# Attention scores as four 32-row products per query tile, one head to a PSUM bank

## The chip, the cores and the metric

The kernel runs on one core of one Trainium2 chip. The metric is the device time of one execution in microseconds (us). Time before: 1463.14 us, the median of 3 runs (1463.08 to 1464.67).

## What is computed

A cross-attention layer with a feed-forward part, and behind it a mixture of eight experts, for 4 x 2048 tokens of 512 numbers. The change touches only the scores of the attention:

```python
q = (x @ Wq + bq).reshape(B, N, 16, 32)      # B 4, N 2048: 16 heads of 32 numbers
k = (y @ Wk + bk).reshape(B, 77, 16, 32)     # 77 context rows for each of the 4 batches
scores = jnp.einsum('bnhd,bmhd->bhnm', q, k) / sqrt(32)
attn = softmax(scores, axis=-1)
out = einsum('bhnm,bmhd->bnhd', attn, v).reshape(B, N, 512)
x = x + relu(out @ W1 + b1) @ W2 + b2        # then layernorm, top-1 of 8 experts
```

## The kernel before

The tokens are worked in 16 blocks (`NBLK`) of 512 (`BLK`), each of 4 sub-tiles (`SUB`) of 128 tokens; four blocks in a row (`BPB`) share one context of `M` = 77 rows. Every large product is done in float32r as three products of split operands: high by high, high by low, low by high (`split3`, L599).

One block goes through these steps on TensorE: transposes of the normalised input (`XT`, L984), the queries (`Q`, L1016, four chunks of 128 features, so four heads each), the scores (`S`, L1042), transposes of the probabilities (`PT`, L1117), attention by values (`AV`, L1153), the hidden layer (`H`, L1201) and the output layer (`YA` and `Y`, L1223). The steps are written out by hand in one list (L273 to L532); every engine walks the same list and does its own part of each step, in that order. The scores of block b+1 are put between the output products of block b (L502 to L514): four groups g = 0 to 3, each a chunk of four heads, and behind each group a half of an output product, and for g = 0 and 1 also the queries of group g+2.

A group of scores before the change is four steps, one for each sub-tile s of 128 tokens. The keys stand in a tile `kbd` in which the four heads are laid out block-diagonally: rows 32h to 32h+31 hold the keys of head h in columns 77h to 77h+76, and zeros elsewhere. So one product of 128 rows by `SC` = 308 columns gives all four heads of a sub-tile, and three such products (L1042) fill one PSUM bank. There are 16 x 4 x 4 x 3 = 768 of them.

Behind them VectorE takes the negated maximum of each head (`dve_s`, L1051). In groups 0 and 2 (`ON_ACT`) ScalarE computes the exponentials and their sums head by head (`act_s`, L1084: 16 instructions of 77 columns per group). In groups 1 and 3 VectorE first subtracts the maximum (`dve_sub`, L1071), and ScalarE then does the whole group in one instruction (`act_soft`, L1092), with the sums on VectorE (L1100). VectorE then takes the reciprocals (`dve_sum`, L1105), GpSimd multiplies the probabilities by them (`pool_soft`, L1111), and TensorE transposes them. The transposes of the second pair of groups begin with two that need group 2 alone (`CA`), and these are the sixth and seventh transposing steps of a block (L283 to L288).

The eight PSUM banks are given out in the order of the list (L574 to L588): each step that writes a bank takes the one given up the longest ago and waits for its last reader (`own_bank`, L590).

`kbd` is zeroed by GpSimd at the start (L791), filled by ScalarE for the first context (`act_kcopy`, L815), and refilled from a DRAM copy of the split keys (`sp_kstore` L697, `sp_kload` L704) three times, by four DMAs each. On the queue of SyncE the load of W2 stands behind the store of the keys (L338, L339).

Of the kernel before, what the change touches and what calls it, by code (L numbers as in the profile page):

```python
# [27 lines left out]
P = 128  # L28
D = 512
# [21 lines left out]
SCP = (SC + 63) // 64 * 64  # L51
# [24 lines left out]
def xattn_moe_kernel(nc, A, out):  # L76
    region = nc.dram_tensor("region", [NE * REG + P, ROW], F32).ap()
    k_parts = nc.dram_tensor("k_parts", [P, 2, KD, NB * M], F32).ap()
# [28 lines left out]
    kbd, _ = sb("kbd", [P, 2, KD, SCP], F32R)  # L107
# [65 lines left out]
    k_hl = staged("k_hl", [P, 2, KD, NB * M], F32R)  # L173
# [15 lines left out]
    assert 4 * NE * D <= size([P, 2, KD, SCP], F32) + size([P, 2, NP, NC, P], F32)  # L189
# [54 lines left out]
    with ExitStack() as ctx:  # L244
        bank = [ctx.enter_context(nc.psum_tensor(f"bank{i}", [P, 512], F32)) for i in range(8)]

        def sem(name):
# [7 lines left out]
        st_k, st_v, ld_k, ld_v = sem("st_k"), sem("st_v"), sem("ld_k"), sem("ld_v")  # L255
# [8 lines left out]
            "act_wq dve_wq act_w1 pool_w1 act_w2 dve_w2 act_kbd dve_tri "  # L264
# [86 lines left out]
        step("VSTORE", 0)  # L351
        step("CONV_W1", 0)
# [3 lines left out]
        for s in range(SUB - 1):  # L356
            step("S", 0, 0, s)
        step("QLO", 0, 1)
        step("Q", 0, 2)
        step("S", 0, 0, SUB - 1)  # L360
        step("CONV_W1", 1)
        for s in range(SUB):
            step("S", 0, 1, s)
# [4 lines left out]
        for s in range(SUB):  # L368
            step("S", 0, 2, s)
# [3 lines left out]
        for s in range(SUB):  # L373
            step("S", 0, 3, s)
# [9 lines left out]
        for b in range(NBLK):  # L384
            last = b == NBLK - 1
            if (b + 1) % BPB == 0 and not last:
                step("KLOAD", (b + 1) // BPB)
# [75 lines left out]
            if last:  # L463
                step("GELU")
                step("PAD_LOAD")
                step("YA", b, 0)
                step("Y", b, 0)
                step("YA", b, 1)
                step("Y", b, 1)
                step("YA", b, 2)  # L470
                step("TT", b, 0)
                step("TTOUT", b, 0)
                step("Y", b, 2)
                step("TT", b, 1)
                step("TTOUT", b, 1)
                step("YA", b, 3)
                step("TT", b, 2)
                step("TTOUT", b, 2)
                step("Y", b, 3)
            else:  # L480
                prep = b - PREP0 if PREP0 <= b < PREP0 + NE else None
                step("DRAIN")
                step("YA", b, 0)
                for s in range(SUB):
                    step("XB", b + 1, s)
                step("Y", b, 0)
                for s in range(2):
                    step("XT", b + 1, s)
                step("YA", b, 1)
                for s in range(2, SUB):  # L490
                    step("XT", b + 1, s)
                if prep is not None:
                    step("E2_RAW", prep)
                    step("E1_RAW", prep)
                step("Y", b, 1)

                for m in range(2):
                    step("Q", b + 1, m)
                    step("QLO", b + 1, m)
                if prep is not None:  # L500
                    step("E2_HIGH", prep)
                for g, (first, y) in enumerate((("YA", 2), ("Y", 2), ("YA", 3), ("Y", 3))):  # L502
                    for s in range(SUB):
                        step("S", b + 1, g, s)
# [34 lines left out]
        def score_done(b, g, s):  # L539

            mine, name = (ON_ACT, "act_es") if g in ON_ACT else (ON_DVE, "dve_sub")
            return S[name], SUB * (len(mine) * b + mine.index(g)) + s + 1


        def group_of(p, i):
# [8 lines left out]
            "S": lambda b, g, s: score_done(b, g, s),  # L554
# [139 lines left out]
        def sp_kstore(sp):  # L694
            sp.wait_ge(S["act_k"], KD)
            sp.wait_ge(S["dve_k"], KD)
            sp.dma_start(k_parts, f32(k_hl[:])).then_inc(st_k, 16)  # L697

        def sp_kload(sp, i):
            sp.wait_ge(st_k, 16)  # L700
            sp.wait_ge(S["pe_s"], KD * SUB * BPB * i)
            for h in range(HG):
                q = slice(HD * h, HD * h + HD)
                sp.dma_start(f32(kbd[q, :, :, M * h:M * h + M]).rearrange("p s g k -> p (s g) k"),  # L704
                             k_parts[q, :, :, M * i:M * i + M].rearrange("p s g k -> p (s g) k")).then_inc(ld_k, 16)

# [16 lines left out]
        KLOADS, VLOADS = HG, len(PIECES)  # L723
# [36 lines left out]
        def sp_ebload(sp):  # L760
            sp.wait_ge(S["pe_s"], KD * SUB * NBLK)
# [45 lines left out]

        def act_kcopy(act):

            act.wait_ge(S["pool_zero"], 1)  # L810
            act.wait_ge(S["act_k"], KD)
            act.wait_ge(S["dve_k"], KD)
            for h in range(HG):
                q = slice(HD * h, HD * h + HD)
                act.activation(kbd[q, :, :, M * h:M * h + M], k_hl[q, :, :, 0:M], ACT.Identity).then_inc(S["act_kbd"], 1)  # L815
# [35 lines left out]
        def act_kp(act, m):  # L851
# [7 lines left out]
            act.activation(k_hl[:, 0, m, :], k_f[:, m, :], ACT.Identity).then_inc(S["act_k"], 1)  # L859

        def dve_klo(dve, m):
            dve.wait_ge(S["act_k"], m + 1)
            dve.tensor_tensor(k_hl[:, 1, m, :], k_f[:, m, :], f32(k_hl[:, 0, m, :]), ALU.subtract
                              ).then_inc(S["dve_k"], 1)
# [180 lines left out]
        def dve_s(dve, b, g, s):  # L1045

            dve.wait_ge(S["pe_s"], SUB * (KD * b + g) + s + 1)
            if b and s == 0 and g in ON_ACT:
                dve.wait_ge(S["act_es"], SUB * (len(ON_ACT) * (b - 1) + ON_ACT.index(g) + 1))
            p = grouped(of("S", b, g, s)[:, 0:SC], HG)  # L1050
            dve.tensor_reduce(mx[:, SUB * g + s, :], p, AX, ALU.max, negate=True).then_inc(S["dve_max"], 1)  # L1051
            if g in ON_DVE:
                if s:
                    dve_sub(dve, b, g, s - 1)
                if s == SUB - 1:
                    drip(1)
                    dve_sub(dve, b, g, s)
# [9 lines left out]
        def dve_sub(dve, b, g, s):  # L1067
            if b and s == 0:
                dve.wait_ge(S["pe_pt"], NC * NP * b)
            dve.wait_ge(S["dve_max"], SUB * (KD * b + g) + s + 1)  # L1070
            dve.tensor_tensor(grouped(probs(g)[:, s, :], HG), grouped(of("S", b, g, s)[:, 0:SC], HG),  # L1071
                              spread(mx[:, SUB * g + s, :], M), ALU.add).then_inc(S["dve_sub"], 1)

        def act_s(act, b, g, s):
            if g not in ON_ACT:
                return
            if b == 0 and s == 0:
                act.wait_ge(S["dve_tri"], 1)
            if b and s == 0:
                act.wait_ge(S["pe_pt"], NC * NP * b)  # L1080
                act.wait_ge(S["dve_rc"], KD * (b - 1) + g + 1)
            act.wait_ge(S["dve_max"], SUB * (KD * b + g) + s + 1)
            for h in range(HG):
                ins = act.activation(probs(g)[:, s, M * h:M * h + M], of("S", b, g, s)[:, M * h:M * h + M], ACT.Exp,  # L1084
# [4 lines left out]
        def act_soft(act, b, g):  # L1089
            if g in ON_DVE:  # L1090
                act.wait_ge(score_done(b, g, SUB - 1)[0], score_done(b, g, SUB - 1)[1])
                act.activation(probs(g), probs(g), ACT.Exp).then_inc(S["act_exp"], 1)  # L1092

        def dve_sum(dve, b, g):
            i = KD * b + g
            if g in ON_ACT:
                dve.wait_ge(score_done(b, g, SUB - 1)[0], score_done(b, g, SUB - 1)[1])
# [22 lines left out]
        def act_pt(act, b, pr, c):  # L1120
            j = NC * pr + c
            if b == 0 and j == 0:
                act.wait_ge(st_k, 16)
                act.wait_ge(S["act_kbd"], HG)
# [585 lines left out]
        def pool_store(pool, t):  # L1710
# [10 lines left out]
            "KCOPY": {"act": act_kcopy},  # L1721
# [3 lines left out]
            "KSTORE": {"sp": sp_kstore},  # L1725
# [6 lines left out]
            "KLOAD": {"sp": sp_kload},  # L1732
# [152 lines left out]
```

## Time and profile before

| | us |
|---|---|
| median of 3 runs | 1463.14 |
| the profiled execution | 1461.93 |
| its span | 1460.1 |
| TensorE busy (matmul) | 1439.2 |
| VectorE busy | 1037.0 |
| ScalarE busy | 756.9 |
| GpSimd busy | 416.0 |
| score products, L1042, 768 of them | 118.7 |

Busy time is the union of the recorded spans of an engine's instructions; a matmul's record reaches past the start of the next, so the distance between two starts, not the length of a record, is what one costs in a row. PE is TensorE's matmul, PEld its load of weights, DVE is VectorE, ACT ScalarE, POOL GpSimd, SPq the DMA issues of SyncE's queue.

### The profile page before, as it was taken

Reading aid. Unit: us, or ns where it says so; the run is one execution under the profiler, and the core shown is the slowest. Engines: PE = TensorE matmul, PEld = TensorE weight load, DVE = VectorE, ACT = ScalarE, POOL = GpSimd, SP = SyncE. Lnnn points to the kernel's source line nnn. Section 1 sums busy time; section 2 is a strip of 40 time slices with the busy share of each in tenths; the row PEclk is TensorE's granted clock in tenths of the full one; section 3 lists DMA queues with packets and bytes.
Section 4 is the critical chain, followed back from the end, with each engine's and each line's share of the span. In section 5 each row is a group of like instructions: output and inputs, shape, how many; then the busy total and the mean of one; then the engine's idle time right before and its main releaser. Section 6 shows DMA issues by size and latency. Waiting matters only on the chain.

```text
span 1460.1 us, 23469 instructions
## 1 busy us (share of the span) xinstructions
PE 1439.2 (99%) x7704; PEld 1203.9 (82%) x7704; DVE 1037.0 (71%) x2522; ACT 756.9 (52%) x2096; POOL 416.0 (28%) x306
## 2 busy tenths in 40 slices
PE   8999999999999999999999999999999999999997
PEld 6788887888788888888787888888887878788996
DVE  6768586776868685867768685858576675748666
ACT  6746353645445363536454453635363544547885
POOL 3422222212121312222221213122222213108875
PEclk9999999999999999999999999999999999999999
DMA  8210202121120303130211201130202012357984
GB/s 294 85 58 1 88 1 73 38 79 55 36 88 22 102 7 103 28 99 30 81 43 37 87 23 58 43 91 1 87 1 87 1 44 73 145 174 255 305 257 149
DMA packets 70339, 121.60 MB, mean 83 GB/s; under 512 B 21851, under 2 KB 30308, under 8 KB 69197
## 3 DMA queue, kind: packets, MB, share of 16 engines
q1 hardware_dynamic: 59421, 86.41, 19.5%
q0 software_dynamic: 10800, 33.70, 6.0%
q8 instruction: 65, 1.06, 0.3%
q14 instruction: 53, 0.43, 0.1%
HBM read 75.19 MB, written 46.40 MB: 83 GB/s over the span
## 4 chain that ended last, share of the span: by engine, by line
PE 96%; DVE 2%; ACT 1%; issue 1%; DMA 0%; POOLq 0%; POOL 0%; SPq 0%; DVEq 0%
PE bank L1201 24%; PE bank L1223 24%; PE bank L1016 12%; PE bank L1153 8%; PE bank L1042 7%; PE bank L1623 4%; PE bank L1117 4%; PE bank L1661 3%; PE bank L1607 2%; PE bank L1298 2%; PE bank L984 2%; PE bank L1276 1%; DVE actH L1134 1%; ACT actH L1128 1%; PE bank L847 1%
## 5 line engine op out<-in xcount | busy, mean ns | idle before, releaser
L1223 PE MATMUL bank<-w,actH 128*128 128x512 f32 x1536 | 372.1, 393 | 0.0
L1201 PE MATMUL bank<-actA,w 128*128 128x512 f32 x1536 | 370.4, 394 | 0.0
L1201 PEld LDWEIGHTS bank<-actA,w 128*128 128x128 f32 x1536 | 284.2, 188 | 61.0
L1223 PEld LDWEIGHTS bank<-w,actH 128*128 128x128 f32 x1536 | 283.0, 188 | 55.9
L1111 POOL TENSOR_TENSOR E<-E,rc 128x1232 f32<-128x1232 f32 x64 | 144.1, 2252 | 423.3 <-DVE rc L1105 423.3
L1373 POOL DMA_INDIRECT region<-rows,pos x64 | 63.7, 996 | 456.6 <-DVE pos L1367 418.2
L1208 ACT ACTIVATE actH<-bank,b 128x512 fp32r<-128x512 f32 x128 | 88.4, 691 | 189.4 <-PE bank L1201 189.4
L1016 PE MATMUL bank<-actA,wq 128*128 128x512 f32 x768 | 182.4, 390 | 0.0
L1084 ACT ACTIVATE E<-bank,mx 128x77 f32<-128x77 f32 x512 | 157.8, 362 | 34.9 <-DVE mx L1051 34.9
L1016 PEld LDWEIGHTS bank<-actA,wq 128*128 128x128 f32 x768 | 144.1, 188 | 30.3 <-issue 0.5
L1030 DVE SCALAR_TENSOR_TENSOR actQ<-bank,bq,actQ 128x512 fp32r<-128x512 f32 x64 | 48.0, 750 | 158.5 <-ACT actQ L1025 158.5
L1213 DVE TENSOR_TENSOR actH<-bank,actH 128x512 fp32r<-128x512 f32 x128 | 88.2, 689 | 55.7 <-ACT bank L1209 55.0
L1153 PE MATMUL bank<-actH,vbd 128*128 128x512 f32 (+1 forms) x480 | 122.0, 400 | 4.2 <-DVE actH L1134 4.2
L1084 ACT ACTIVATION_READ_ACCUMULATOR E<-bank,mx 128x1 f32 x512 | 124.5, 243 | 0.0
L1042 PE MATMUL bank<-kbd,actQ 128*128 128x308 f32 x768 | 118.7, 303 | 0.0
L1042 PEld LDWEIGHTS bank<-kbd,actQ 128*128 128x128 f32 x768 | 113.9, 188 | 5.7 <-issue 0.5
L1051 DVE TENSOR_REDUCE mx<-bank 128x4 f32<-128x308 f32 x256 | 110.4, 471 | 6.8 <-PE bank L1042 6.8
L1025 ACT ACTIVATE actQ<-bank,bq 128x512 fp32r<-128x512 f32 x64 | 44.1, 689 | 125.1 <-PE bank L1016 125.0
L1153 PEld LDWEIGHTS bank<-actH,vbd 128*128 128x128 f32 (+1 forms) x480 | 86.5, 188 | 25.7 <-DVE actH L1134 6.9
L1134 DVE TENSOR_TENSOR actH<-bank,actH 128x512 fp32r<-128x512 f32 (+1 forms) x160 | 98.7, 676 | 11.5 <-ACT actH L1128 11.5
L1006 POOL TENSOR_TENSOR rows<-rows,b2bc 128x512 f32<-128x512 f32 x64 | 84.7, 1335 | 52.5 <-DMA rows<-in_x 43.7
L989 ACT ACTIVATE actA<-bank 128x512 fp32r<-128x512 f32 x64 | 34.7, 596 | 107.7 <-PE bank L984 107.7
(172 smaller groups left out, 2108.3 us busy)
## 6 DMA issues: line engine op xcount, KB each, us to landing
rowB<-region SPq DMA_DIRECT2D x71, 258.0 KB
xn<-in_x SPq DMA_DIRECT2D x64, 256.0 KB, 2.9
rows<-in_x SPq DMA_DIRECT2D x64, 256.0 KB, 3.5
w_raw<-in_W SPq DMA_DIRECT2D x2, 2048.0 KB, 10.5
e_raw<-in_E SPq DMA_DIRECT2D x16, 256.0 KB, 3.2
region<-padrow SPq DMA_DIRECT2D x9, 258.0 KB, 2.2
e_parts<-e_high SPq DMA_DIRECT2D x8, 256.0 KB, 2.0
e_parts<-e_low SPq DMA_DIRECT2D x8, 256.0 KB, 2.3
```

What stands on the lines that cost most here:

```text
L1006: nc.gpsimd.tensor_tensor(r, r, b2bc[:], ALU.add).then_inc(S["pool_xb"], 1)
L1016: mm = pe.matmul(p[:], w, a, start=k == 0 and j == 0, stop=k == KD - 1 and j == 2)
L1042: mm = pe.matmul(p[:, 0:SC], q, k, start=j == 0, stop=j == 2)
L1051: dve.tensor_reduce(mx[:, SUB * g + s, :], p, AX, ALU.max, negate=True).then_inc(S["dve_max"], 1)
L1084: ins = act.activation(probs(g)[:, s, M * h:M * h + M], of("S", b, g, s)[:, M * h:M * h + M], ACT.Exp, bias=mx[:, SUB * g + s, h:h + 1], a ...
L1111: nc.gpsimd.tensor_tensor(e, e, r, ALU.mult).then_inc(S["pool_p"], 1)
L1134: dve.tensor_tensor(actH[0:CH[c], 1, j % SLOTS, :], of("PT", b, pr, c)[0:CH[c], :], f32(actH[0:CH[c], 0, j % SLOTS, :]), ALU.subtract).the ...
L1153: mm = pe.matmul(p[:], v, w, start=c == mine[0] and t == 0, stop=c == mine[-1] and t == 2)
L1201: mm = pe.matmul(p[:], w, a, start=k == 0 and j == 0, stop=k == KD - 1 and j == 2)
L1208: act.activation(actH[:, 0, m, :], p[:], ACT.Relu, bias=b1[:, m:m + 1])
L1213: dve.tensor_tensor(actH[:, 1, m, :], of("H", b, m)[:], f32(actH[:, 0, m, :]), ALU.subtract).then_inc(S["dve_h"], 1)
L1223: mm = pe.matmul(p[:], a, w, start=m == 0 and j == 0, stop=m == MF - 1 and j == 2)
```

## The change

`kbd` is gone. The split keys stay in `k_hl`, now a tile of its own with `KW` = 320 columns for all four contexts, its 12 last columns zeroed. The zeroing of `kbd`, the copies into it, its store and its twelve loads are gone, with their semaphores; the load of W2 moves behind the loads and the store of the first values on SyncE's queue.

A group of scores is now four steps by head, not by sub-tile. Each takes a bank, but TensorE does the whole group at the last of them: for each of the 4 sub-tiles and each of the 3 split products, four products of 32 rows by `KS` = 78 columns, one per head, each to the bank of its head. So 48 products per group where there were 12, and 3072 in all. The one increment of the semaphore comes after the last. VectorE and ScalarE read by head: the maxima of the four sub-tiles of one head, the subtraction likewise, the exponentials in as many instructions of the same size.

```diff
-        step("KSTORE")
-        step("W2_LOAD")
         step("CONV_WQ", 1)
         step("VP", 0)
-        step("KCOPY")
...
         step("VSTORE", 0)
+        step("W2_LOAD")
         step("CONV_W1", 0)
...
-            if (b + 1) % BPB == 0 and not last:
-                step("KLOAD", (b + 1) // BPB)
...
-            z(f32(kbd[:])).then_inc(S["pool_zero"], 1)
+            z(f32(k_hl[:, :, :, NB * M:KW])).then_inc(S["pool_zero"], 1)
...
-        def pe_s(pe, b, g, s):
-            p = own_bank(pe, "S", b, g, s)
-            if s == 0:
-                pe.wait_ge(S["dve_q"], KD * b + g + 1)
-                pe.wait_ge(S["act_kbd"], HG)
-                if b >= BPB:
-                    pe.wait_ge(ld_k, 16 * KLOADS * (b // BPB))
-            for j, (q, k) in enumerate(split3([actQ[:, h, g, P * s:P * s + P] for h in range(2)],
-                                              [kbd[:, h, g, 0:SC] for h in range(2)])):
-                mm = pe.matmul(p[:, 0:SC], q, k, start=j == 0, stop=j == 2)
+        def pe_s(pe, b, g, h):
+
+
+            own_bank(pe, "S", b, g, h)
+            if h < HG - 1:
+                return
+            pe.wait_ge(S["dve_q"], KD * b + g + 1)
+            if b == 0:
+                pe.wait_ge(S["pool_zero"], 1)
+                pe.wait_ge(S["dve_k"], g + 1)
+            i = b // BPB
+            for s in range(SUB):
+                for j, (q, k) in enumerate(((0, 0), (0, 1), (1, 0))):
+                    for h in range(HG):
+                        r = slice(HD * h, HD * h + HD)
+                        mm = pe.matmul(of("S", b, g, h)[:, KS * s:KS * s + KS], actQ[r, q, g, P * s:P * s + P],
+                                       k_hl[r, k, g, M * i:M * i + KS], start=j == 0, stop=j == 2)
             mm.then_inc(S["pe_s"], 1)
...
+        def dve_s(dve, b, g, h):
+
+            dve.wait_ge(S["pe_s"], KD * b + g + 1)
...
+            dve.tensor_reduce(maxima(g, h), scores(b, g, h), AX, ALU.max, negate=True).then_inc(S["dve_max"], 1)
```

## Rows read from the trace of the kernel before

**Rows 1.** The page: TensorE's busy time, and its granted clock in 40 slices.
```profile
PE 1439.2 (99%) x7704; PEld 1203.9 (82%) x7704; DVE 1037.0 (71%) x2522; ACT 756.9 (52%) x2096; POOL 416.0 (28%) x306
...
PEclk9999999999999999999999999999999999999999
```

**Rows 2.** The page: the chain that ended last, shares by engine and line.
```profile
PE 96%; DVE 2%; ACT 1%; issue 1%; DMA 0%; POOLq 0%; POOL 0%; SPq 0%; DVEq 0%
PE bank L1201 24%; PE bank L1223 24%; PE bank L1016 12%; PE bank L1153 8%; PE bank L1042 7%; PE bank L1623 4%; PE bank L1117 4%; PE bank L1661 3%; PE bank L1607 2%; PE bank L1298 2%; PE bank L984 2%; PE bank L1276 1%; DVE actH L1134 1%; ACT actH L1128 1%; PE bank L847 1%
```

**Rows 3.** Groups by line and shape: score products, count | busy us, mean ns | idle before.
```profile
L1042 PE MATMUL bank<-kbd,actQ 128*128 128x308 f32 x768 | 118.7, 303 | 0.0
L1042 PEld LDWEIGHTS bank<-kbd,actQ 128*128 128x128 f32 x768 | 113.9, 188 | 5.7 <-issue 0.5 <-DVE actQ L1030 0.4
```

**Rows 4.** Timeline of PE around group 0, block 8: start us, length us, count.
```profile
650.94 5.60 PE L1016 MATMUL bank<-actA,wq 128*128 128x512 f32 x24
656.38 1.85 PE L1042 MATMUL bank<-kbd,actQ 128*128 128x308 f32 x12
658.07 2.92 PE L1223 MATMUL bank<-w,actH 128*128 128x512 f32 x12
```

**Rows 5.** Timeline of PE and PEld, 149 us: four products of 16 rows, L1312.
```profile
148.75 0.39 PE L1201 MATMUL bank<-actA,w 128*128 128x512 f32 x1
149.07 0.42 PE L1312 MATMUL bank<-ident,csb 16*128 16x16 f32 x4
149.41 1.43 PE L1201 MATMUL bank<-actA,w 128*128 128x512 f32 x5
...
149.07 0.32 PEld L1312 LDWEIGHTS bank<-ident,csb 16*128 16x128 f32 x4 [0.35 <-issue]
149.41 1.23 PEld L1201 LDWEIGHTS bank<-actA,w 128*128 128x128 f32 x6
```

**Rows 6.** The line L1312 over the whole run: count, duration min/median/max, idle before.
```profile
L1312 PEld LDWEIGHTS bank<-ident,csb x60: 132/136/138, 149.1 to 1265.4; 16*128 16x128 f32 x60
L1312 PE MATMUL bank<-ident,csb x60: 207/208/229, 149.1 to 1265.4; 16*128 16x16 f32 x60
...
  issue: 5.3, 15
```

**Rows 7.** Timeline of PE, block 8: the shortest pairs of load and product.
```profile
635.33 0.24 PE L1347 MATMUL bank<-cum,ones 128*128 128x8 bf16 x4
635.43 3.00 PE L1201 MATMUL bank<-actA,w 128*128 128x512 f32 x12
```

**Rows 8.** Timeline of PEld: two full weight loads whose products have one column.
```profile
621.45 0.30 PEld L1398 LDWEIGHTS bank<-onesf,e_acc 128*128 128x128 f32 x2
621.67 2.62 PEld L1201 LDWEIGHTS bank<-actA,w 128*128 128x128 f32 x12
```

**Rows 9.** Timeline of all engines from group 3 of block 8 to its transposes.
```profile
675.16 1.85 PE L1042 MATMUL bank<-kbd,actQ 128*128 128x308 f32 x12
...
675.78 0.90 DVE L1051 TENSOR_REDUCE mx<-bank 128x4 f32<-128x308 f32 x2 [0.23 <-PE bank L1042]
...
676.85 2.93 PE L1223 MATMUL bank<-w,actH 128*128 128x512 f32 x12
...
678.14 0.85 DVE L1071 TENSOR_TENSOR E<-bank,mx 128x308 f32<-128x308 f32 x2
678.91 0.24 DVE L1105 RECIPROCAL rc<-sm 128x16 f32<-128x16 f32 x1
...
679.24 2.25 POOL L1111 TENSOR_TENSOR E<-E,rc 128x1232 f32<-128x1232 f32 x1 [1.34 <-DVE rc L1105]
679.62 3.22 PE L1117 MATMUL bank<-ident,E 128*128 128x128 f32 x28
```

**Rows 10.** Timeline of PE, block 0: its sixth transposing step.
```profile
45.23 1.06 PE L1117 MATMUL bank<-ident,E 128*128 128x128 f32 x8 [0.18 <-POOL E L1111]
```

**Rows 11.** Timeline of the first 75 us: work removed or moved by the change.
```profile
0.75 2.23 POOL L790 MEMSET kbd<- 128x2560 f32 x1 [0.29 <-POOLq L1878]
...
18.91 6.02 PE L1016 MATMUL bank<-actA,wq 128*128 128x512 f32 x24
...
19.82 2.97 ACT L815 ACTIVATE kbd<-k_hl 32x616 fp32r<-32x616 f32 x4 [0.88 <-DVE k_hl L863]
20.17 0.43 SPq L664 DMA_DIRECT2D w_raw<-in_W  x1
...
36.95 0.42 SPq L729 DMA_DIRECT2D v_parts<-v_hl  x1
```

**Rows 12.** DMA issues: KB, us to landing; and the line that first reads W2.
```profile
w_raw<-in_W SPq DMA_DIRECT2D x2, 2048.0 KB, 10.5
kbd<-k_parts SPq DMA_DIRECT2D x12, 77.0 KB, 2.5
...
L924 ACT ACTIVATE w<-w_raw x4: 1062/1075/1103, 66.4 to 73.8; 128x1024 fp32r<-128x1024 f32 x4
```

More of the change, by code:

```diff
@@ L50 @@
 SC = HG * M
-SCP = (SC + 63) // 64 * 64
+KS = M + 1
+KW = (NB * M + 63) // 64 * 64
 NP = KD // 2
@@ L188, in xattn_moe_kernel @@
     b2e = at("b2e", [P, NE, D], F32, vbd_at)
-    assert 4 * NE * D <= size([P, 2, KD, SCP], F32) + size([P, 2, NP, NC, P], F32)
+    assert 4 * NE * D <= size([P, 2, KD, KW], F32) + size([P, 2, NP, NC, P], F32)
     o = [w2_at]
@@ L351, in xattn_moe_kernel @@
         step("VSTORE", 0)
+        step("W2_LOAD")
         step("CONV_W1", 0)
         step("Q", 0, 1)
-        for s in range(SUB - 1):
-            step("S", 0, 0, s)
+        for h in range(HG):
+            step("S", 0, 0, h)
         step("QLO", 0, 1)
         step("Q", 0, 2)
-        step("S", 0, 0, SUB - 1)
         step("CONV_W1", 1)
-        for s in range(SUB):
-            step("S", 0, 1, s)
+        for h in range(HG):
+            step("S", 0, 1, h)
         step("QLO", 0, 2)
@@ L367, in xattn_moe_kernel @@
         step("SUM", 0, 0)
-        for s in range(SUB):
-            step("S", 0, 2, s)
+        for h in range(HG):
+            step("S", 0, 2, h)
         step("QLO", 0, 3)
@@ L372, in xattn_moe_kernel @@
         step("SUM", 0, 1)
-        for s in range(SUB):
-            step("S", 0, 3, s)
+        for h in range(HG):
+            step("S", 0, 3, h)
         step("EXP", 0, 3)
@@ L502, in xattn_moe_kernel @@
                 for g, (first, y) in enumerate((("YA", 2), ("Y", 2), ("YA", 3), ("Y", 3))):
-                    for s in range(SUB):
-                        step("S", b + 1, g, s)
+                    for h in range(HG):
+                        step("S", b + 1, g, h)
                     if prep is not None and g == 0:
@@ L692, in sp_xload @@
                 sp.dma_start(rows[b % 2][:, s, 0:D], src).then_inc(ld_x[b % 2][s], 16)
[L694 to L705, printed above, removed]
         def sp_vload(sp, i, part):
@@ L721, in sp_vload @@
                              ).then_inc(ld_v, 16)
-        KLOADS, VLOADS = HG, len(PIECES)
+        VLOADS = len(PIECES)
         def sp_vstore(sp, i):
@@ L760, in sp_ebload @@
         def sp_ebload(sp):
-            sp.wait_ge(S["pe_s"], KD * SUB * NBLK)
+            sp.wait_ge(S["pe_s"], KD * NBLK)
             sp.wait_ge(S["pe_av"], 3 * NP * NBLK)
@@ L806, in dve_masks @@
             dve.tensor_copy(ones[:], c_raw[:, P:2 * P]).then_inc(S["dve_tri"], 1)
[L808 to L815, printed above, removed]
         def pe_gate(pe):
@@ L1045, in dve_s @@
[L1045 to L1051, printed above, removed]
+        def pe_s(pe, b, g, h):
[9 more added lines that the diff above has]
+                for j, (q, k) in enumerate(((0, 0), (0, 1), (1, 0))):
+                    for h in range(HG):
+                        r = slice(HD * h, HD * h + HD)
+                        mm = pe.matmul(of("S", b, g, h)[:, KS * s:KS * s + KS], actQ[r, q, g, P * s:P * s + P],
+                                       k_hl[r, k, g, M * i:M * i + KS], start=j == 0, stop=j == 2)
+            mm.then_inc(S["pe_s"], 1)
@@ new lines, in scores, with maxima @@
+        def scores(b, g, h):
+            return of("S", b, g, h)[:, 0:SUB * KS].rearrange("p (s k) -> p s k", s=SUB)[:, :, 0:M]
+        def maxima(g, h):
+            return mx[:, SUB * g:SUB * g + SUB, h]
+        def dve_s(dve, b, g, h):
+            dve.wait_ge(S["pe_s"], KD * b + g + 1)
+            if b and h == 0 and g in ON_ACT:
+                dve.wait_ge(S["act_es"], HG * (len(ON_ACT) * (b - 1) + ON_ACT.index(g) + 1))
+            dve.tensor_reduce(maxima(g, h), scores(b, g, h), AX, ALU.max, negate=True).then_inc(S["dve_max"], 1)
@@ L1052, in dve_s @@
             if g in ON_DVE:
-                if s:
-                    dve_sub(dve, b, g, s - 1)
-                if s == SUB - 1:
+                if h:
+                    dve_sub(dve, b, g, h - 1)
+                if h == HG - 1:
                     drip(1)
-                    dve_sub(dve, b, g, s)
+                    dve_sub(dve, b, g, h)
         def probs(g):
@@ L1065, in by_head, with dve_sub, act_s @@
             return ap.rearrange("p s (h k) -> p s h k", h=HG)
-        def dve_sub(dve, b, g, s):
-            if b and s == 0:
+        def dve_sub(dve, b, g, h):
+            if b and h == 0:
                 dve.wait_ge(S["pe_pt"], NC * NP * b)
[L1070 to L1074, printed above, removed]
+            dve.wait_ge(S["dve_max"], HG * (KD * b + g) + h + 1)
+            dve.tensor_tensor(probs(g)[:, :, M * h:M * h + M], scores(b, g, h), spread(maxima(g, h), M), ALU.add
+                              ).then_inc(S["dve_sub"], 1)
+        def act_s(act, b, g, h):
             if g not in ON_ACT:
                 return
-            if b == 0 and s == 0:
+            if b == 0 and h == 0:
                 act.wait_ge(S["dve_tri"], 1)
-            if b and s == 0:
+            if b and h == 0:
                 act.wait_ge(S["pe_pt"], NC * NP * b)
                 act.wait_ge(S["dve_rc"], KD * (b - 1) + g + 1)
-            act.wait_ge(S["dve_max"], SUB * (KD * b + g) + s + 1)
-            for h in range(HG):
-                ins = act.activation(probs(g)[:, s, M * h:M * h + M], of("S", b, g, s)[:, M * h:M * h + M], ACT.Exp,
+            act.wait_ge(S["dve_max"], HG * (KD * b + g) + h + 1)
+            for s in range(SUB):
+                ins = act.activation(probs(g)[:, s, M * h:M * h + M], scores(b, g, h)[:, s, :], ACT.Exp,
                                      bias=mx[:, SUB * g + s, h:h + 1],
```

28 lines of the change are left out of this document (11 added, 17 removed).

## Prediction

> **What bounds the kernel now.** I read the page's busy times first: TensorE has 1439.2 us of 1460.1, at a granted clock of 1.0 (the 2.4 GHz level) in every slice [rows 1]. The chain that ended last runs 96% over TensorE, 7% of it through the score products [rows 2]. So TensorE's own sequence is the time: what a score group costs there counts in full, 64 times (16 blocks, 4 groups), and a saving on another engine counts nothing unless TensorE waits for it. The groups by line give 768 score products and a weight load for each, with 0.0 and 5.7 us of idle time before them [rows 3]. The timeline of one group gives the pace: 24 query products take 5.44 us from first start to the first score (0.227 each), the 12 score products 1.69 us to the next start (0.141 each) [rows 4]. The 204 columns between 512 and 308 cost 0.086 us, 0.42 ns a column. Loads are hidden here.
>
> **What a group costs after.** Before, from the start of the last product ahead to the first start behind: 0.23 + 1.69 = 1.92 us. After, 48 products with 48 loads stand there. Four terms:
>
> *Entry.* The only products of few rows in this trace are the transposes of 16 rows. The last full product ahead of them starts at 148.75, their first load at 149.07: 0.32 us, where a full product would have followed in 0.23, and the load would have run beside the product ahead. PEld shows the gap as 0.35 us ended by "issue" [rows 5], 5.3 us in 15 such places [rows 6]. No semaphore is named. I read it as the array emptying before products with another number of rows. 0.32 us.
>
> *First load.* Two full loads whose products have a single column start 0.22 us apart over two, 0.11 each [rows 8]: that is a 128-column load's own pace. Nothing hides the first one: 0.11 us.
>
> *Exit.* The four small transposes take 0.42 us to the end of the last record, which is 0.21 long [rows 5, 6], so the last starts at 149.28; the next full load comes 0.13 us later at 149.41 [rows 5]. A product of 78 columns is 62 columns longer, 0.03 us, and the load before the first full product again costs 0.11. Together 0.27 us.
>
> *Pace.* 47 steps of p. The trace has no products of 32 rows in different row groups, so p is bounded from both sides. Below: four bf16 products with their loads start within 0.10 us, 0.025 each [rows 7]; nothing in the trace is issued faster. Above: one load after the other, 0.11 us each [rows 8]. Between them lies the pace of the 16-row loads, all in the same rows: (0.32 - 0.136) / 3 = 0.061 us [rows 5, 6]. The change alternates the four heads, so four consecutive loads go to four different sets of 32 rows and four consecutive products to four banks. If these sets work side by side, four loads take the time of one: 0.11 / 4 = 0.028. I take 0.028, next to the lowest row, because [rows 4] already show a load running beside a product under way. If in each set the load also had to wait for that set's own product (78 x 0.42 ns = 0.033 us), p would be 0.143 / 4 = 0.036.
>
> The group costs 0.70 + 47p: 2.02 us at 0.028, so +0.10 us per group, +6 us over 64. At 0.025 it is 1.88 (-3 us), at 0.036 2.39 (+30 us).
>
> The Trainium skill, "TensorE: Matmul & The Clock Gate", LDWEIGHTS, says that a load's time is its columns divided by 1.2 GHz, whatever its rows: an estimate of 107 ns here. The full loads agree (0.11), the 16-row ones don't (0.061), so by the rule alone the one-at-a-time case below would sit at its dear end. Part 3 of the same page says that loads overlap products under way only in a differing row group; no run here shows it yet.
>
> **The wait that is added.** Before, VectorE could begin a group after the first of four banks. Now all four are complete only at the end of the group. Ahead of groups 0 to 2 nothing waits that closely. Group 3 is different. Before: its products start at 675.16, the first maximum at 675.78 (0.62 us), the last subtraction ends at 678.99, reciprocals of group 2 behind them at 678.91, then GpSimd 679.24 to 681.49, which is 6.33 us after 675.16 [rows 9]. Queued behind the maxima on VectorE are thus the subtractions and the reciprocals on which group 2's probabilities wait, and behind the subtractions ScalarE's exponentials of group 3. TensorE starts transposing at 679.62, 0.109 apart ((3.22 - 0.27) / 27), and its 21st product, the first that needs group 2, comes at 681.80 [rows 9]: 0.31 us of slack, the same pattern in blocks 1 to 15. In block 0 there is none, TensorE waits 0.18 us there [rows 10].
>
> After: the last product starts 0.11 + 1.32 = 1.43 us behind the group's first load; its record is some 0.24 us (between 0.208 for 16 columns and 0.303 for 308 [rows 3, 6]), and 0.04 to VectorE as before (0.28 + 0.30 to 0.62). So the maxima start at 1.71 instead of 0.62, 1.09 us later, and GpSimd ends at 7.42. TensorE, whose way to the transposes is 1.70 instead of 1.69, is there at 6.65. With 0.1 us of hand-over it waits 0.87 us per block, 14 us over 16 blocks. A longer p moves both sides alike. What is late next, VectorE's low parts of the transposed probabilities, is some 1.1 us later too and TensorE 0.9, so at most 0.2 us more per block; I leave that in the range.
>
> **What is removed or moved.** All at nothing. GpSimd's 2.23 us memset and ScalarE's 2.97 us of copies lie beside other work: the query products run from 18.91 to 24.8 while the copies are made [rows 11]. The twelve reloads (2.5 us to land) are issued once group 3 of a context's last block is through, half a block's output and hidden products before the next scores; TensorE's idle time names none of them [rows 3, 12]. W2's load moves on SyncE's queue from 20.17 to about 37.4, behind the value loads and their store at 36.95; it needs 10.5 us, so it lands by 48, and its first reader starts at 66.4 [rows 11, 12]. The token loads behind it are 0.4 us later. If the cover of W2 were gone it would cost what it lands past 66.4; 18 us are left. The number and size of VectorE's and ScalarE's instructions stays.
>
> **Sum.** +6 +14 = +20 us on the profiled execution's 1461.9 (its span and 1.8 us around it), 1482; the median of the runs shown lies 1.2 us above the profiled one, so 1483.
>
> **Rivals.**
>
> *One load at a time, in the small rows' pace* (p = 0.061): for it, the only products of few rows in the trace go at this pace; against, they all use the same rows. 0.70 + 2.87 = 3.57 us, +1.65 x 64 = +106, with the wait +120: 1583.
>
> *The change doesn't do what it says*: products of different heads don't run side by side at all and each load costs its full 0.11 (p = 0.11). 5.87 us, +253, with the wait +267: 1730. For it: a full load is no cheaper for a product of one column.
>
> *Faster*: the entry and exit gaps belong to those transposes alone and not to the number of rows. Then entry is 0.23, exit 0.14 and the first load hidden: 0.37 + 47 x 0.025 = 1.55 us, -0.37 x 64 = -24, with the wait of 14 us: 1453. It decides from a group cost below 1.92 - 0.22 = 1.70 us, where the saving passes the wait. Against it: [rows 6] show the same gap in all 15 places, both ways.
>
> The Trainium skill, "TensorEngine Tiling (Array Packing)", Key Properties, says that changing the tiling mode drains the engine and that different tiles load and multiply in parallel. By the first, the faster rival falls; by the second, both dear rivals do. The first agrees with the gaps of 0.32 and 0.13 us; no row shows the second.
>
> **How the numbers follow.** Side by side, with the drain (p 0.025 to 0.036: 1474 to 1507, likeliest 1483): 0.55. One at a time or partly so (1507 to 1600): 0.16. No gain from rows (about 1730): 0.13. Faster by over 0.2% (down to 1453): 0.10. Within 0.2%, about what a measurement of this kernel can tell from no change, between these: 0.06. The range reaches from 1455 to 1592, leaving out the dearest rival and the ends of its neighbours. Faster 0.10, same 0.06, slower 0.84.
>
> **What would show it.** In the changed kernel: the distance from the last full product to the first score load (0.32), from the last score product to the next full load (0.16), the start-to-start pace of the 3072 products (0.028), the first maximum of group 3 at 1.7 us behind its first load, and an idle time of TensorE at the transposing line, put down to GpSimd, of some 14 us where there are 0.2. A pace of 0.06 or more makes the prediction far too low; gaps like any other product's make it too high.

## The result, and the profile after

The changed kernel takes 1477.35 us (median of 4 runs, 1476.07 to 1480.55) against 1463.11 for the kernel before on the same chip: ratio 1.0099, 95% interval 1.0080 to 1.0118, so 14 us slower. Its profiled execution has a span of 1474.3 us, 14.1 more than before.

The page of the changed kernel: busy times and the granted clock in 40 slices, to be read against [rows 1].

```profile
PE 1437.9 (98%) x10008; PEld 1181.5 (80%) x10008; DVE 1039.7 (71%) x2522; ACT 750.5 (51%) x2092; POOL 413.5 (28%) x306
...
PEclk9999999999999999999999999999999999999999
```

TensorE has 2304 more products, is busy 1.3 us less and spans 14.1 us more. The time went into idle time of TensorE, not into its products. The groups by line and shape of the changed kernel (count | busy us, mean ns | idle us before and its releaser), where [rows 3] had 118.7 us:

```profile
L1020 PE MATMUL bank<-k_hl,actQ 32*128 32x78 f32 x3072 | 98.4, 280 | 2.6 <-ACT E L1069 1.3 <-DVE actQ L1002 1.3
```

**One group.** The timeline of TensorE in the changed kernel, group 0 of block 8 (start us, length us), against [rows 4]:

```profile
659.88 5.60 PE L988 MATMUL bank<-actA,wq 128*128 128x512 f32 x24
665.42 1.54 PE L1020 MATMUL bank<-k_hl,actQ 32*128 32x78 f32 x48
666.88 3.01 PE L1207 MATMUL bank<-w,actH 128*128 128x512 f32 x12
669.73 2.88 PE L988 MATMUL bank<-actA,wq 128*128 128x512 f32 x12
```

24 query products take 5.54 us to the first score product, 0.10 more than before: the entry, 0.32 instead of 0.23. The group takes 1.46 to the next start instead of 1.69. The twelve output products behind it take 2.85. In the kernel before the same twelve start at 658.07 [rows 4], and the next row of its timeline is

```profile
660.83 1.52 PE L1016 MATMUL bank<-actA,wq 128*128 128x512 f32 x6
```

so they took 2.76 there: after the change the first of them waits 0.09 for its load. The whole piece, from the first query product to the start behind the twelve output products, is 5.44 + 1.69 + 2.76 = 9.89 us before and 5.54 + 1.46 + 2.85 = 9.85 after. A group costs 0.04 us less than before, where I forecast 0.10 more.

**Group 3 and its consumers.** The timeline of all engines of the changed kernel in block 8, against [rows 9]:

```profile
684.10 1.54 PE L1020 MATMUL bank<-k_hl,actQ 32*128 32x78 f32 x48
...
685.69 0.87 DVE L1036 TENSOR_REDUCE mx<-bank 128x4 f32<-128x308 f32 x2 [1.16 <-PE bank L1020]
...
688.01 0.85 DVE L1056 TENSOR_TENSOR E<-bank,mx 128x308 f32<-128x308 f32 x2
688.44 2.35 PE L1102 MATMUL bank<-ident,E 128*128 128x128 f32 x20
688.78 0.24 DVE L1090 RECIPROCAL rc<-sm 128x16 f32<-128x16 f32 x1
688.90 1.24 ACT L1077 ACTIVATE E<-E 128x1232 f32<-128x1232 f32 x1 [2.02 <-DVE E L1056]
...
689.11 2.25 POOL L1096 TENSOR_TENSOR E<-E,rc 128x1232 f32<-128x1232 f32 x1 [2.24 <-DVE rc L1090]
...
691.50 1.06 PE L1102 MATMUL bank<-ident,E 128*128 128x128 f32 x8 [0.72 <-POOL E L1096]
```

The maxima start 1.59 us behind the group's first product (0.62 before), and VectorE itself now waits 1.16 us. GpSimd ends at 691.36, and the sixth transposing step, which could have followed at 690.62, starts at 691.50: 0.72 us recorded as idle, 0.88 between starts. What follows on TensorE, first in the kernel before, then in the changed one:

```profile
682.67 0.60 PE L1276 MATMUL bank<-ident,rows 128*128 128x128 f32 x4
683.17 3.68 PE L1153 MATMUL bank<-actH,vbd 128*128 128x512 f32 x15
```

```profile
692.40 0.60 PE L1260 MATMUL bank<-ident,rows 128*128 128x128 f32 x4
692.76 3.70 PE L1137 MATMUL bank<-actH,vbd 128*128 128x512 f32 x15
696.29 0.60 PE L1260 MATMUL bank<-ident,rows 128*128 128x128 f32 x4
```

Before, the first value product stood 0.50 us behind the start of the four transposes ahead of it, now 0.36: a little is given back there. From the first transpose to the first value product it is 683.17 - 679.62 = 3.55 us before and 692.76 - 688.44 = 4.32 after, 0.77 more in a block. The line's waits over the run, from its own view (idle us, times):

```profile
  POOL E L1096: 12.2, 16
```

**Block 0.** The timeline of TensorE in the changed kernel:

```profile
25.80 1.54 PE L1020 MATMUL bank<-k_hl,actQ 32*128 32x78 f32 x48
...
30.84 1.54 PE L1020 MATMUL bank<-k_hl,actQ 32*128 32x78 f32 x48 [0.56 <-ACT E L1069]
...
36.62 1.54 PE L1020 MATMUL bank<-k_hl,actQ 32*128 32x78 f32 x48 [1.29 <-DVE actQ L1002]
...
41.70 1.54 PE L1020 MATMUL bank<-k_hl,actQ 32*128 32x78 f32 x48 [0.77 <-ACT E L1069]
...
49.69 1.07 PE L1102 MATMUL bank<-ident,E 128*128 128x128 f32 x8 [1.41 <-POOL E L1096]
```

From the first scores to that sixth transposing step it takes 23.89 us; before it took 45.23 - 24.77 = 20.46. Each group here waits until all of its four banks are free, or for low parts of queries that are behind the group's maxima on VectorE.

**The balance.** The first scores start 1.0 us later, at 25.80 instead of 24.77 (not shown to be the change's: the kernel before with two steps moved, below, starts as late); block 0 takes 3.4 us more; the transposes of 15 blocks at 0.77 are 11.6 us; 60 groups at -0.04 are -2.4. That makes 13.6 of the 14.1, taking block 8 for all of blocks 1 to 15.

### The profile page after: what moved, and what is told of

Its sections match the earlier page's. It is cut to its first block, busy times and chain, and to the rows that moved or that the text cites. A ratio compares the mean times of both kernels' runs of the same rounds, so it can differ in the third digit from the quotient of the medians.

```text
span 1474.3 us, 28075 instructions
## 1 busy us (share of the span) xinstructions
PE 1437.9 (98%) x10008; PEld 1181.5 (80%) x10008; DVE 1039.7 (71%) x2522; ACT 750.5 (51%) x2092; POOL 413.5 (28%) x306
## 4 chain that ended last, share of the span: by engine, by line
PE 90%; DVE 5%; POOL 2%; issue 1%; ACT 1%; DMA 0%; POOLq 0%; SPq 0%; DVEq 0%; ACTq 0%
PE bank L1185 24%; PE bank L1207 22%; PE bank L988 11%; PE bank L1137 8%; PE bank L1020 6%; PE bank L1607 4%; PE bank L1645 3%; POOL E L1096 2%; PE bank L1591 2%; PE bank L1282 2%; PE bank L956 2%; DVE mx L1036 2%; DVE E L1056 2%; PE bank L1102 2%; PE bank L1260 1%
## 5 line engine op out<-in xcount | busy, mean ns | idle before, releaser
L1207 PE MATMUL bank<-w,actH 128*128 128x512 f32 x1536 | 378.0, 397 | 0.0
L1020 PEld LDWEIGHTS bank<-k_hl,actQ 32*128 32x128 f32 x3072 | 91.0, 186 | 25.7 <-issue 25.7
L1020 PE MATMUL bank<-k_hl,actQ 32*128 32x78 f32 x3072 | 98.4, 280 | 2.6 <-ACT E L1069 1.3
L1102 PE MATMUL bank<-ident,E 128*128 128x128 f32 (+1 forms) x640 | 78.1, 273 | 12.2 <-POOL E L1096 12.2
```

Of the source, the lines that this page charges most:

```text
L1020: mm = pe.matmul(of("S", b, g, h)[:, KS * s:KS * s + KS], actQ[r, q, g, P * s:P * s + P], k_hl[r, k, g, M * i:M * i + KS], start=j == 0, s ...
L1102: mm = pe.transpose(p[0:CH[c], P * s:P * s + P], E[:, pr, s, P * c:P * c + CH[c]], ident[:])
L1207: mm = pe.matmul(p[:], a, w, start=m == 0 and j == 0, stop=m == MF - 1 and j == 2)
```

## Experiments

Each was timed beside the kernel before on the same chip; "ratio" is to that, with its 95% interval. They ran on three chips, where the kernel before took 1463.9, 1459.5 and 1459.8 us, so kernels timed on different chips are compared by ratio.

### The wait without the products

```diff
-            p = own_bank(pe, "S", b, g, s)
-            if s == 0:
...
+            own_bank(pe, "S", b, g, s)
+            if s < SUB - 1:
+                return
...
+            for s in range(SUB):
...
+            mm.then_inc(S["pe_s"], SUB)
```

> The kernel before with its 128-row products, but all four sub-tiles of a group done at the last of the four steps, with one increment behind the last product: the wait of the change without its products. Theory (the loss of the change is the later start of group 3 on VectorE, and bank waits in block 0; the products themselves cost nothing): the maxima start some 1.9 us behind the group's first product, against 0.62 before and 1.6 in the changed kernel, so TensorE waits about 1.0 us per block at the transposes, 16 us, and block 0 loses some 3 us at its banks: about 1481, no faster than the changed kernel. Rival (the loss is in the small products and the gaps around them): 1463, like before.

Measured: 1488.91 us, ratio 1.0170 (1.0153 to 1.0187), +25 us. The timeline of TensorE of this kernel, block 8 and then block 0:

```profile
693.47 1.85 PE L1044 MATMUL bank<-kbd,actQ 128*128 128x308 f32 x12
...
697.92 2.35 PE L1119 MATMUL bank<-ident,E 128*128 128x128 f32 x20
701.16 1.07 PE L1119 MATMUL bank<-ident,E 128*128 128x128 f32 x8 [0.89 <-POOL E L1113]
```

```profile
28.56 1.85 PE L1044 MATMUL bank<-kbd,actQ 128*128 128x308 f32 x12
33.94 3.42 PE L1044 MATMUL bank<-kbd,actQ 128*128 128x308 f32 x12 [3.53 <-ACT E L1086]
```

The wait of the change is there with the old products: 0.89 us recorded, 1.06 between starts (3.24 from 697.92 against 20 x 0.109), a little more than in the changed kernel because the group itself is longer. 15 x (1.06 - 0.11), with what the changed kernel gives back behind it (0.88 - 0.77) taken off, are 14 us, near the forecast of 16. The other 8 us over the forecast are in block 0, and come with my edit: its list has group 0's last step behind the third query chunk, so the whole group moved there (28.56 against 24.77), and group 1 behind it waits 3.53 us for banks. Behind that wait its twelve products take 3.42 us and not 1.85, because the granted clock fell there (us, TensorE busy (count), granted clock, DMA share, GB/s):

```profile
33.00:39.80 6.80, 5.86 (x19) 0.50 0.38 81
```

So part of the 8 us is clock and not waiting. The rival, that the loss lies in the small products, falls: the loss at the transposes is there without them.

### Taking the wait away

```diff
                     for h in range(HG):
                         step("S", b + 1, g, h)
+                        if g == 3 and h == 1:
+                            step("SUM", b + 1, 2)
...
-                    if g:
+                    if g in (1, 2):
                         step("SUM", b + 1, g - 1)
```

> The changed kernel with the reciprocals of group 2 (and with them GpSimd's product) put between the maxima of the second and the third head of group 3, in blocks 1 to 15. If the wait at the transposes is the only one, it goes and 15 x 0.78 = 12 us come back: about 1465. Theory as the trace is read: GpSimd then ends in time, but ScalarE's exponentials of group 3 still stand ahead of the copies of the transposed probabilities, so the first value product waits in its place (about 0.6 to 0.8 us per block): 1474 to 1478, under 4 us gained.

Measured: 1479.44 us, ratio 1.0104 (1.0087 to 1.0121). The timeline of TensorE, block 8:

```profile
689.43 3.22 PE L1104 MATMUL bank<-ident,E 128*128 128x128 f32 x28
...
693.85 3.70 PE L1139 MATMUL bank<-actH,vbd 128*128 128x512 f32 x15 [0.77 <-DVE actH L1120]
```

The 28 transposes run through, and the first value product waits 0.77 us instead. So the theory holds that the wait only moves. I had expected it between the changed kernel's time and up to 4 us less; it came out at or slightly above the changed kernel (ratio 1.0104 against 1.0099, within the intervals).

With the exponentials of group 3 moved as well:

```diff
-                    step("EXP", b + 1, g)
+                    if g < 3:
+                        step("EXP", b + 1, g)
...
                 step("PT", b, 0, c)
+                if b and c == 2:
+                    step("EXP", b, 3)
```

> The same, and the exponentials of group 3 put behind the third copy of transposed probabilities on ScalarE, in blocks 1 to 15. Theory: both consumers are then in time, the 12 us come back: 1464 to 1467, with no idle time of TensorE at the transposes or the value products outside block 0. Rival (something else than these two queues delays TensorE after group 3): above 1472.

Measured: 1472.47 us, ratio 1.0061 (1.0044 to 1.0078): some 5.5 us regained, not 12, at the edge of what the rival said.

```profile
685.40 3.22 PE L1107 MATMUL bank<-ident,E 128*128 128x128 f32 x28
688.46 0.60 PE L1265 MATMUL bank<-ident,rows 128*128 128x128 f32 x4
689.26 3.70 PE L1142 MATMUL bank<-actH,vbd 128*128 128x512 f32 x15 [0.20 <-DVE actH L1123]
```

The value products start 0.80 us behind the transposes' last group, 0.44 more than the 0.36 of the changed kernel (692.40 to 692.76): still a wait, now on VectorE.

> The kernel before with the same two moves. It has 0.3 us of slack at both places, so nothing is to be gained: 1463, within 1 us. If it gains as much as the changed kernel does by them, the moves are worth something by themselves and say nothing about the change.

Measured: 1469.78 us, ratio 1.0043 (1.0027 to 1.0060): not equal but slower, by 6 us. The two moves cost the kernel before 0.3 to 0.4 us per block. In block 8, 0.14 of it is at the first value product (0.64 us behind the four transposes ahead of it, against 0.50) and 0.19 at the eighth transposing step, which needs group 3's probabilities (1.66 us behind the start of six value products, against 1.47 in the kernel before): the late exponentials make the copies and the sums behind them late. So by themselves they are a loss; together with the change's late maxima they are the smaller of two losses. Against this kernel, the changed one with the same moves is only 2.7 us slower. Its start tells what the scatter of a start is: nothing ahead of block 1 differs from the kernel before, and yet its first queries start at 19.93 where [rows 11] have 18.91:

```profile
19.93 6.04 PE L1021 MATMUL bank<-actA,wq 128*128 128x512 f32 x24
```

Two more moves, to see whether the waits that are left can be taken away too:

```diff
-                    drip(DRIP.get(kind, 0))
+                    drip(0 if kind == "Y" and i[1] == 3 or kind == "PT" and i[1] == 0 and i[2] < 2 else DRIP.get(kind, 0))
...
+        step("QLO", 0, 2)
         for h in range(HG):
             step("S", 0, 1, h)
-        step("QLO", 0, 2)
```

> The changed kernel with the early reciprocals and the late exponentials, and two more moves: VectorE's statistics of the block before (0.69 us) go behind its low parts of the first three transposed chunks, and in block 0 the low part of the third query chunk goes ahead of group 1's maxima. Theory: the wait of 0.33 us per block at the first value product goes (5 us) and 1.3 us of block 0, from 1472.5: about 1466, no better than the kernel before, since 2 us of block 0 remain and the groups themselves gain only 0.03 us each. Rival (VectorE is full there, the wait only moves to the next consumer): 1471 or more.

Measured: ratio 1.0065 (1.0051 to 1.0079), no gain over the version before it. Its waits of TensorE (idle us in total, times, longest):

```profile
PE bank L1025 <- ACT E L1074: 2.5, 2, 1.9
PE bank L1107 <- POOL E L1101: 2.4, 15, 0.2
```

The wait at the first value product is gone; in its place the eighth transposing step waits for group 3's probabilities (2.4 us recorded in 15 places; in the timeline 1.78 us from the start of six value products, against 1.49 in the version before: 0.3 lost), and in block 0 a bank wait of 1.9 us stands where the queries' low part stood. Behind that wait the granted clock also fell in this execution (0.51 from 43.9 to 47.3 us), so that six 512-column products took 4.37 us where the changed kernel's take 2.71. The rival was right: around group 3 VectorE has no room, and what is taken from one consumer is missing at the next. No version beat the kernel before.

### What entering and leaving small products costs

```diff
+            if s == 0:
+                pe.matmul(p[:, 0:M + 1], actQ[0:HD, 0, g, 0:P], kbd[0:HD, 0, g, 0:M + 1], start=True, stop=True)
```

> The kernel before with one more product in each of the 64 groups, ahead of the twelve: 32 rows by 78 columns, into the first bank, overwritten right behind (its result is not used). Theory (entering and leaving 32-row products empties the array): 0.32 us from the last full product to it, 0.21 from it to the next full load and 0.11 for that load, where 0.23 stood: +0.41 us, 64 times, +26: about 1489. Rival (a small product costs only its own load or columns, 0.03 to 0.11 us): 1465 to 1470.

Measured: ratio 1.0186 (1.0170 to 1.0201), +27 us, 0.42 per group. The timeline of TensorE and the line's own view:

```profile
690.51 0.30 PE L1041 MATMUL bank<-kbd,actQ 32*128 32x78 f32 x1
690.74 1.95 PE L1044 MATMUL bank<-kbd,actQ 128*128 128x308 f32 x12
692.53 2.93 PE L1225 MATMUL bank<-w,actH 128*128 128x512 f32 x12
```

```profile
L1041 PE MATMUL bank<-kbd,actQ x64: 270/299/300, 25.2 to 1261.3; 32*128 32x78 f32 x64
...
  issue: 22.4, 63
```

The twelve products behind it take 1.79 us instead of 1.69: 0.10 for their first load. A single 32-row product costs as much as three score products of 308 columns. So entry and exit, 0.42 us together, are paid each time TensorE goes from 128 rows to 32 and back, 64 times here, for one product as for 48.

### The pace inside a group

```diff
-            for s in range(SUB):
+            for h0, s in [(h0, s) for h0 in (0, 2) for s in range(SUB)]:
...
-                    for h in range(HG):
+                    for h in (h0, h0 + 1):
```

> The changed kernel with the heads alternated two at a time: all products of heads 0 and 1, then all of heads 2 and 3; same 48 products, banks and increment. Theory (what sets the pace is one load of 0.112 us in each set of rows, and sets work side by side): 24 steps of 0.112 instead of 12, +1.34 us per group, +86: about 1563. Rival (the products are issued at a pace of their own, 0.028 each): 1477, as with four.

Measured: 1572.51 us, ratio 1.0771 (1.0754 to 1.0787), +113. The forecast was +86 on top of the change's 14, so 100.

The same with `for h0 in range(HG)` and `(h0,)`:

> The changed kernel with one head after the other: twelve products of head 0, then of head 1 and so on, all else as it is. Theory (a load costs 0.112 us in its rows, whatever its number of rows): 48 steps, +4.0 us per group, +258: about 1735. Rival (small loads go at the 0.061 us of the 16-row transposes): 48 x 0.061 = 2.9 against 1.34, +1.6 us per group, +102: about 1579.

Measured: 1798.9 us, ratio 1.2321 (1.2302 to 1.2340), +339. The forecast was 258 and 14. Timelines of TensorE, two heads at a time, then one:

```profile
645.85 2.45 PE L1020 MATMUL bank<-k_hl,actQ 32*128 32x78 f32 x48
648.23 4.60 PE L1207 MATMUL bank<-w,actH 128*128 128x512 f32 x12
```

```profile
650.79 5.29 PE L1020 MATMUL bank<-k_hl,actQ 32*128 32x78 f32 x48
656.02 5.17 PE L1207 MATMUL bank<-w,actH 128*128 128x512 f32 x12
```

Two things come together. *The groups*: 2.38 us to the next start with two heads, against 1.46 with four, +0.92 and not +1.34. Between the two halves the queue reaches ahead: the products of the second pair begin while those of the first are still under way, since they use other rows. In the timeline the pace falls out as 48 products in 2.45 - 0.28 = 2.17 us. So sets of rows do work side by side. One set by itself shows its pace in the run with one head at a time: eight loads of head 0, and seven of them, in two windows of its timeline of weight loads,

```profile
650.79 0.96 PEld L1020 LDWEIGHTS bank<-k_hl,actQ 32*128 32x128 f32 x8 [0.35 <-issue]
650.79 0.85 PEld L1020 LDWEIGHTS bank<-k_hl,actQ 32*128 32x128 f32 x7 [0.35 <-issue]
```

are 0.11 us apart. Within a set a load and its product take 0.11 us, and not the 0.061 of the rival: the first theory, with an overlap between sets that I had not foreseen. *The clock*: the output products behind take 4.60 us instead of 2.85. The windows of these stretches (core 0: us, TensorE busy (count), granted clock, DMA share, GB/s), two heads at a time:

```profile
645.90:648.20 2.30, 2.30 (x49) 1.00 0.00 0
648.30:652.70 4.40, 4.40 (x12) 0.61 0.00 0
```

In a full-speed stretch an output product takes 0.227 us, here up to 0.427: the 1.2 GHz level. Over the run the line's mean goes from 397 ns in the changed kernel to 433 with two heads and 485 with one (the groups by line and shape, in this order):

```profile
L1207 PE MATMUL bank<-w,actH 128*128 128x512 f32 x1536 | 378.0, 397 | 0.0
```

```profile
L1207 PE MATMUL bank<-w,actH 128*128 128x512 f32 x1536 | 423.7, 433 | 0.0
```

```profile
L1207 PE MATMUL bank<-w,actH 128*128 128x512 f32 x1536 | 492.2, 485 | 0.0
```

The clock explains what the pace doesn't: with two heads 59 us (64 x 0.92) over the changed kernel's 14 leave 40. The output products are busy 423.7 - 378.0 = 46 us longer than in the changed kernel and the queries 3.5; against that, VectorE has more time, and TensorE waits 7.2 us less at the transposes (5.0 against 12.2) and 2.6 less at the scores. That makes 40. With one head the mean clock is 0.90 and the groups themselves run partly at the lower level, so its total gives no clean price. Where the clock stayed up, a group takes 4.22 us to the next start (639.31 to 643.53), 2.76 more than with four heads side by side and not 4.0: here too each head begins before the one ahead is through.

### What lowers the clock

```diff
-            for s in range(SUB):
+            for s in [*range(SUB), *range(SUB)]:
```

> The changed kernel with the 48 products of each group done twice (the second time overwrites the first): four heads side by side as in the change, but 24 steps long. It asks what lowers the granted clock behind the groups of two heads, where twelve output products took 4.6 us instead of 3.0. If it is that only some of the four sets of 32 rows are busy, the clock stays at its upper level: 12 more steps of 0.112 us per group, +1.34, 64 times, +86 above the changed kernel: ratio to before about 1.068. If it is the length of the stretch of small products (2.6 us here, 2.2 with two heads), output products go at 0.43 each behind many groups and 40 us or more come on top: ratio 1.09 or more.

Measured: 1585.36 us, ratio 1.0867 (1.0845 to 1.0889), +126, of which 14 are the change's and 86 the doubled steps; of the 26 left, the output products are busy 27 longer (405.0 against 378.0) and the wait at the transposes is 1.5 shorter. That is between the two theories, nearer the second. The timeline of TensorE, block 7 to 8:

```profile
654.16 4.61 PE L1207 MATMUL bank<-w,actH 128*128 128x512 f32 x12
658.70 2.88 PE L1020 MATMUL bank<-k_hl,actQ 32*128 32x78 f32 x96
661.51 3.02 PE L1207 MATMUL bank<-w,actH 128*128 128x512 f32 x12
```

The 96 products take 2.81 us to the next start, 1.35 more than 48, which confirms 0.112 us per step of four heads. Behind some groups of 2.8 us the output products are slow (4.61), behind others they aren't (3.02), with all four sets of rows busy: 17 of the 62 stretches of twelve products behind a group take over 4.4 us here, 31 of 62 with two heads. So neither theory stands alone. The clock falls behind longer stretches of such products even with four heads side by side, and with two heads a stretch of 2.4 us costs more at the output products (46 us) than 2.8 us with four (27). What TensorE's clock counts in them isn't settled by these runs. In the changed kernel, with 1.46 us per group, the clock did not fall before the last 7 us of the run (mean 0.998, as in the kernel before).

## Why the prediction was right, and where not

The forecast was 1483, slower, with two causes: the drain (the array emptying at entry and exit) at +6 us, and the wait at +14. 1477 came out, and both are there, but the drain does no more than use up what the faster pace saves: a group comes out 0.04 us cheaper, not 0.10 dearer, and the loss is the wait, block 0 and a start 1.0 us later. The range of 1455 to 1592 was so wide that the time inside it says little. By the forecast's steps:

- *What bounds the kernel.* Right: 3072 products for 768, and the time moved by what TensorE's sequence lost.
- *Entry.* 0.32 us forecast from the 16-row transposes; 0.32 measured (5.54 for 24 products), and the added single product pays it too.
- *First load, 0.11.* Wrong, one of two mis-sized terms of the group. The record of the first product starts with the group and the whole group of 48 takes 1.54 us to the end of its last record of 0.28, so 1.26 from first to last start, where I had 0.11 + 1.32. The eleven steps of 0.112 behind the first make 1.23 of that: 0.02 or 0.03 is left for the first load. That is 0.09 us, 64 times: 6 us of the forecast's 20. The other 0.08 lies in the 47 steps of 0.028: the four products of one step start almost together, so eleven full steps count and not eleven and three quarters; 5 us more.
- *Exit.* 0.27 forecast, of which 0.16 to the next full load and 0.11 for it. Measured 0.20 (1.46 - 1.26) and 0.09 to 0.10: 0.30. The words "both ways" in the forecast's case against a faster kernel were more than [rows 6] have: they show the gap at the entry only, and [rows 5] one exit.
- *Pace.* 0.028 forecast from one full load spread over four sets of rows; 1.26 / 47 = 0.027 measured. The choice of the cheap end was right for the reason given; pairs and doubled groups show it. The two dear rivals fall, and so does the 0.036 of a load that waits for its own set's product: one set alone goes at 0.11 us a step, not 0.143. So a load runs beside a product in the same rows too, as it does before the change, where 128-row loads are hidden behind 128-row products [rows 4]. What the prediction took from the Trainium skill ("TensorE: Matmul & The Clock Gate", Part 3), that loads overlap only products in other rows, is not so here.
- *The Trainium skill's* statement that a load takes its number of columns divided by 1.2 GHz, whatever its rows ("TensorE: Matmul & The Clock Gate", LDWEIGHTS), holds closely for the 32-row loads here: by it a load of 128 columns is an estimated 107 ns, measured are 0.11 us from load to load in one set of rows and 0.112 us for a step of four heads. The 0.061 us of the 16-row transposes, which I had set against it, was no measure for these products. Its rule that a change of the tiling mode drains the engine ("TensorEngine Tiling (Array Packing)", Key Properties) agrees with the entry of 0.32 and with the 0.42 us of a single product.
- *The wait.* 0.87 us per block forecast, 0.88 between starts measured (0.72 recorded as idle), at the place and by the queue named: the wait for the last bank, VectorE's maxima 1.6 us behind the group's first product (1.71 forecast), reciprocals, GpSimd. Shown by the kernel before with the wait alone.
- *Block 0* was left out but for that wait. It lost 3.5 us at banks and queries: there the groups stand close to each other, and waiting for four free banks at once costs what before was waited for one by one. I had said that ahead of groups 0 to 2 nothing waits that closely; that is true of blocks 1 to 15 only.
- *What is removed or moved*, at nothing: TensorE's waits name no key, no zeroing and no W2. The start of 1.0 us later is also in the kernel before with two steps moved.

With the group at its measured price, the sum would have been -3 + 14 = 11, and with block 0's 2.6 us besides the wait about 14, as measured. So the forecast came close partly by luck: 9 us too much for the groups were partly made up by block 0 and the later start, which it had at nothing.

## What to carry to other kernels

Small products in separate rows are as fast as forecast, and still bought nothing: a group of 48 at 0.027 each replaces 12 at 0.141, but going to 32 rows and back costs some 0.4 us, which uses up nearly the whole saving of a group this short. A longer stretch would spread that cost, but whether it pays is not shown here: with stretches of 2.8 us the clock fell behind some of them. When an engine's work on several banks is made to end at once, follow each consumer of the first bank through its queue; 1 us of later start, where the first consumer had 0.3 us of slack, was 12 of the 14 us lost. And where a wait can be moved away, test the same move on the kernel before: a full engine hands the wait on to the next consumer.

## What the runs showed of the hardware

Stretches of 32-row products lower the granted clock for what follows, though TensorE is recorded as busy throughout: behind 2.4 us with two sets of rows the 512-column products take up to 0.43 us instead of 0.227 (clock 0.61 in that stretch), behind 2.8 us with four sets sometimes, behind 1.46 us with four sets nowhere in the changed kernel's trace. What it is in these stretches that lowers the clock stays open. Products of other rows that stand further back in the list begin before the ones ahead are through: two halves of 24 products, 12 steps of 0.112 us each, would take 2.7 us one after the other, and together took 2.17 from first to last start.
